# A DLRM tower with CIN layers on one core: look-ups in two passes over the tables, and part of the first copies loaded before the last features are written

## The reference

```
e = stack([tbl_f[ids[:, f]] for f in range(39)], axis=1)        # (2048, 39, 32)
conv1 = einsum('bid,bjd,ijk->bkd', e, e, W1)                    # k = 128
hidden1, final1 = conv1[:, :64], conv1[:, 64:]
conv2 = einsum('bid,bjd,ijk->bkd', e, hidden1, W2)              # k = 128
z = sum(concat([final1, conv2], 1), axis=2)                     # (2048, 192)
h = relu(concat([z, dense_ctx], 1) @ W_top1 + b_top1)           # 512
h = relu(h @ W_top2 + b_top2)                                   # 256
y = h @ W_top3                                                  # (2048, 1)
```

## Time and profile before

| | |
|---|---|
| median of 3 runs | 811.2 us (807.7 to 817.63) |
| profiled execution, its own time | 808.5 us |
| its span | 806.6 us |
| mean granted clock of TensorE | 0.966 of full |
| PE busy | 739.2 us (92%) |
| DVE busy | 697.9 us (87%) |
| ACT busy | 572.3 us (71%) |
| POOL busy | 543.3 us (67%) |
| DMA | 179.32 MB, 222 GB/s over the span |

### The profile page before, as it was taken

One profiled execution on the slowest core, in us unless ns is written; L12 is line 12 of the kernel. 1 busy time (PEld: TensorE's weight loads), 2 busy tenths in 40 slices (PEclk: granted clock), 3 DMA queues, 4 the chain that ended last, 5 costly groups with the idle time before them and its releaser, 6 DMA issues.

```text
span 806.6 us, 18279 instructions
## 1 busy us (share of the span) xinstructions
PE 739.2 (92%) x6938; PEld 431.1 (53%) x6938; DVE 697.9 (87%) x1142; ACT 572.3 (71%) x1535; POOL 543.3 (67%) x538
## 2 busy tenths in 40 slices
PE   2991787899999999999999999998999999999997
PEld 1660132375656565655556464655556565656576
DVE  6971986879999999899989898997999999999962
ACT  1330335768888888888887878786888888788883
POOL 6877777777777777777777777777777777700000
PEclk9995986899999999999999999999999999999999
DMA  6738878988898888989898889888898989888500
GB/s 194 233 66 221 241 189 235 254 244 250 253 235 248 239 257 232 262 237 247 228 255 244 243 240 242 241 235 243 232 252 237 252 234 265 248 252 249 158 2 2
DMA packets 135720, 179.32 MB, mean 222 GB/s; under 512 B 105304, under 2 KB 116518, under 8 KB 117648
## 3 DMA queue, kind: packets, MB, share of 16 engines
q1 hardware_dynamic: 111524, 166.84, 71.6%
q0 software_dynamic: 17088, 8.78, 6.6%
q10 hardware_dynamic: 7020, 2.52, 1.2%
HBM read 166.35 MB, written 16.71 MB: 227 GB/s over the span
## 4 chain that ended last, share of the span: by engine, by line
PE 29%; DVE 20%; DMA 20%; ACT 11%; SPq 8%; POOL 6%; issue 6%; ACTq 0%; DVEq 0%; POOLq 0%
DVE blocks L787 18%; DMA copies<-xt 16%; PE hidden L420 14%; SPq L350 7%; PE sums L473 6%; PE sums L447 6%; POOL emb L386 6%; ACT arena L636 5%; DMA xt<-emb 2%; DMA emb<-in_tbl,ids_tile 2%; ACT hid_high L605 2%; PE sums L478 2%; DVE turned L819 2%; ACT xdiag L624 2%; ACT hidden L613 1%
## 5 line engine op out<-in xcount | busy, mean ns | idle before, releaser
L386 POOL DMA_INDIRECT emb<-in_tbl,ids_tile x534 | 543.1, 1017 | 164.8 <-issue 112.5
L787 DVE TENSOR_TENSOR blocks<-copies 117x512 f32<-117x512 f32 x840 | 524.7, 693 | 75.5 <-DMA copies<-xt 59.7
L420 PE MATMUL hidden<-blocks,w_pairs 117*64 117x512 f32 x1792 | 434.6, 614 | 40.3 <-DVE blocks L787 38.4
L636 ACT ACTIVATE arena<-sums 64x480 f32<-64x480 f32 (+2 forms) x936 | 293.0, 313 | 138.6 <-PE sums L447 125.6
L420 PEld LDWEIGHTS hidden<-blocks,w_pairs 117*64 117x64 f32 x1792 | 152.1, 139 | 244.9 <-issue 105.5
L447 PEld LDWEIGHTS sums<-xdiag,turned 64*103 64x103 f32 x2000 | 101.5, 172 | 82.5 <-issue 46.1
L624 ACT ACTIVATE xdiag<-turned 32x468 f32<-32x468 f32 (+1 forms) x256 | 118.8, 464 | 25.7 <-DVE turned L763 22.6
L447 PE MATMUL sums<-xdiag,turned 64*103 64x78 f32 x2000 | 115.4, 262 | 3.3 <-ACT arena L636 2.2
L605 ACT ACTIVATE hid_high<-hidden 32x512 f32<-32x512 f32 x126 | 74.1, 588 | 11.6 <-PE hidden L420 9.7
L473 PE MATMUL sums<-arena,weights 128*64 128x128 f32 x1280 | 78.5, 279 | 0.0
L473 PEld LDWEIGHTS sums<-arena,weights 128*64 128x64 f32 x1280 | 71.1, 139 | 2.4
(11 more groups left out here) (50 smaller groups left out, 258.3 us busy)
## 6 DMA issues: line engine op xcount, KB each, us to landing
copies<-xt SPq DMA_DIRECT2D x448, 312.0 KB
emb<-in_tbl,ids_tile POOLq DMA_INDIRECT x534
xt<-emb SPq DMA_DIRECT2D x32, 152.0 KB
xt<-xt SPq DMA_DIRECT2D x16, 304.0 KB
xt<-emb SPq DMA_DIRECT2D x32, 104.0 KB
blocks<-hot_t SPq DMA_DIRECT2D x6, 512.0 KB, 6.1
xt<-emb SPq DMA_DIRECT2D x32, 56.0 KB
weights<-in_finals SPq DMA_DIRECT2D x1, 1728.0 KB
```

The costliest lines, as they stand in the source:

```text
L386: pool.indirect_dma_start(out=emb[u][:, f * D:(f + 1) * D], out_offset=None, in_=tables[f], in_offset=bass.IndirectOffsetOnAxis(ap=ids_til ...
L420: mm = nc.tensor.matmul(hidden[64 * c:64 * c + 64, k % 2, bank, :], w_pairs[0:ROWS, t, bank * HALF_HID:bank * HALF_HID + HID], blocks[0:RO ...
L636: op = nc.scalar.activation(out[:, :, cols].rearrange("p h (u b) -> p h u b", u=2), g[rows, i], ACT.Copy)
L787: op = nc.vector.tensor_tensor(blocks[0:ROWS, at + c, :], a[:, cols], b[:, cols], ALU.mult)
```

## The change

The 12 look-ups run in another order: j % 6 is the table and j // 6 the half, so the first six look-ups serve samples 0 to 1,023 of all six tables. They no longer skip the 128 samples of tile 0: ScalarE copies these rows into `emb[0]` (a new activation in `copy_rows`, counted in `hot_first`), and POOL's six gathers for them are gone, with the waits of the gathers on `hot_looked`. The ids are loaded in 12 pieces of 1,024 (eight places) instead of six of 2,048 (four places). All six tables are loaded at the start, each to a place of its own; five unpacked tables lie in buffers 2 and 3 of `copies`, the sixth and the raw ones in buffers 6 and 7, so the second place of the ones is buffers 4 and 5. The rows are stored to DRAM in two stores (tiles 1 to 7, tiles 8 to 15) of all six features instead of three stores of two features. On SP, the first two parts of the spill of tile 0 are issued, then, when they have landed, eight loads with those rows of copies 0, 4 and 1 that are already written (`EARLY`, 227 rows of 8 KB), then the last part of the spill, the wait for it, and the rest of the loads. In `spill` the wait for the last part's gathers moves behind the DMA L316.

```diff
-ONES_BEFORE = [2 * c for c in itertools.accumulate([0] + HOT_C)]
+ONES_BEFORE = list(itertools.accumulate([0] + HOT_C + HOT_C))
-INDICES = 4
-TABLES = 4
+INDICES = 8
+TABLES = 5
-COPIES_FREE = LOOKUPS - 8
-ONES_PLACE = [j % 3 if j < COPIES_FREE else 2 if j % 2 == 0 else 0 for j in range(LOOKUPS)]
+TURNED_FREE = LOOKUPS - 3
+ONES_PLACE = [j % 3 if j < LOOKUPS - 1 else 0 for j in range(LOOKUPS)]
+EARLY = {(0, 0): (0, 32), (0, 1): (0, 32), (0, 2): (0, 32), (4, 0): (0, 32), (4, 1): (0, 13),
+         (1, 0): (0, 30), (1, 1): (0, 30), (1, 2): (0, 26)}
...
                 for s in some:
                     part = PARTS[s]
-                    sp.wait_ge(gathered[u][s], 16 * gathers(tile, s))
+                    if s < len(PARTS) - 1:
+                        sp.wait_ge(gathered[u][s], 16 * gathers(tile, s))
                     if s == 0 and tile:
                         sp.wait_ge(hot_rows_loaded[u], 16 * hot_loads(tile))
+                    elif s == 0:
+                        sp.wait_ge(hot_first, N_HOT)
                     if s == len(PARTS) - 1:
                         sp.wait_ge(spilled_first[u], 16 * 2 * (p + 1))
                         sp.dma_start(xt[u, F:F + AGAIN, :, :].rearrange("f h n -> (f h n)").rearrange("(a b) -> a b", a=16),
                                      xt[u, 0:AGAIN, :, :].rearrange("f h n -> (f h n)").rearrange("(a b) -> a b", a=16)
                                      ).then_inc(spilled[u], 16)
+                        sp.wait_ge(gathered[u][s], 16 * gathers(tile, s))
...
-                elif chunk == 1:
-                    sp.wait_ge(hot_looked, COPIES_FREE)
-                elif v in (2, 3):
+                elif chunk == 1 or v in (2, 3):
                     sp.wait_ge(hot_looked, LOOKUPS)
                 for g, r in enumerate(ROTATION[v]):
-                    sp.dma_start(x_copy[v][k % ahead][g::THIRDS, :],
-                                 xt[u, r:r + F, k, :]).then_inc(copied[v][k % ahead], 16)
+                    skip = EARLY[v, g][1] if chunk == 0 and (v, g) in EARLY else 0
+                    sp.dma_start(x_copy[v][k % ahead][g::THIRDS, :][skip:F],
+                                 xt[u, r + skip:r + F, k, :]).then_inc(copied[v][k % ahead], 16)
+
+            def load_early():
+                sp.wait_ge(spilled_first[0], 16 * 2)
+                sp.wait_ge(spilled[0], 16 * 2)
+                sp.wait_ge(cleared, 3)
+                for (v, g), (first, last) in EARLY.items():
+                    r = ROTATION[v][g]
+                    sp.dma_start(x_copy[v][0][g::THIRDS, :][first:last],
+                                 xt[0, r + first:r + last, 0, :]).then_inc(copied[v][0], 16)
 
             def first_tile():
-                for n in range(N_HOT):
-                    index(n)
...
-                    spill(0, 0, [s for s in range(len(PARTS)) if FIRST_SPILLED[s] == n])
+                for j in range(LOOKUPS):
+                    index(j)
...
+                spill(0, 0, range(len(PARTS) - 1))
+                load_early()
+                spill(0, 0, [len(PARTS) - 1])
                 sp.wait_ge(spilled[0], 16 * SPILLS)
...
-            for f in range(F):
-                if f >= AT_ONCE:
-                    pool.wait_ge(hot_looked, (f - AT_ONCE) // A_LOOKUP + 1)
+            for f in range(N_HOT, F):
                 gather(0, f)
             pool.wait_ge(ids_loaded[1], 16)
-            for at, f in enumerate(range(N_HOT, F)):
-                pool.wait_ge(hot_looked, (F - AT_ONCE + at) // A_LOOKUP + 1)
+            for f in range(N_HOT, F):
                 gather(1, f)
...
             def look_up(j):
-                n = j // 2
+                n = j % N_HOT
...
-                        skip = P if j % 2 == 0 and bank == 0 else 0
...
             def copy_rows(j):
-                n, h = j // 2, j % 2
+                n, h = j % N_HOT, j // N_HOT
                 act.wait_ge(hot_summed, j + 1)
+                if h == 0:
+                    nc.scalar.activation(emb[0][:, n * D:(n + 1) * D], sums[:, j % 4, 0:D], ACT.Copy).then_inc(hot_first, 1)
...
-            load_table(0)
-            load_table(1)
+            for n in range(N_HOT):
+                load_table(n)
             for n in range(3):
                 unpack(n)
-                load_table(n + 2)
             act.dma_start(dense_rows[:, :, :], dense).then_inc(dense_loaded, 16)
             for j in range(LOOKUPS):
                 stage(j)
-                if j % 4 == 1 and j > 4:
-                    keep((j - 5) // 4)
+                if j == N_HOT + 1:
+                    keep(0)
                 if j:
                     copy_rows(j - 1)
-                if j % 2 == 0 and j // 2 + 3 < N_HOT:
-                    unpack(j // 2 + 3)
...
+                if j + 3 < N_HOT:
+                    unpack(j + 3)
...
             for j in range(LOOKUPS):
                 indices_to_ones(j)
-                if j % 2 and j // 2 + 2 < N_HOT:
-                    split(j // 2 + 2)
+                if j + 2 < N_HOT:
+                    split(j + 2)
...
-            dve.wait_ge(hot_looked, LOOKUPS - 1)
+            dve.wait_ge(hot_looked, TURNED_FREE)
             turn_x(0, 0)
```

More of the change, by code:

```diff
@@ L138, in build @@
         y_col = sb("y_col", [P, TILES], F32)
-        rows = sb("rows", [P, 2, TILES, 2, D], F32)
+        rows = sb("rows", [P, 2, TILES // 2, N_HOT, D], F32)
         row_number = sb("row_number", [P, 18], F32)
@@ L176, in build @@
         hot_consts_loaded = sem("hot_consts_loaded")
-        hot_raw_loaded = [sem(f"hot_raw_loaded{n}") for n in range(2)]
+        hot_raw_loaded = [sem(f"hot_raw_loaded{n}") for n in range(N_HOT)]
         hot_unpacked = sem("hot_unpacked")
@@ L185, in build @@
         hot_copied = sem("hot_copied")
+        hot_first = sem("hot_first")
         hot_kept = [sem(f"hot_kept{m}") for m in range(2)]
@@ L258, in gathers @@
             part = PARTS[s]
-            each = part.stop - max(part.start, N_HOT)
-            return each * (tile // 2 + 1) if tile % 2 else part.stop - part.start + each * (tile // 2)
+            return (part.stop - max(part.start, N_HOT)) * (tile // 2 + 1)
         def hot_loads(tile):
@@ L266, in loads_done @@
         def loads_done(u, tile, k):
-            return 16 * len(ROTATION[u]) * (tile + 1 if len(x_copy[u]) == 2 else 2 * tile + k + 1)
+            early = len([w for w, _ in EARLY if w == u]) if k == 0 or len(x_copy[u]) == 1 else 0
+            return 16 * (early + len(ROTATION[u]) * (tile + 1 if len(x_copy[u]) == 2 else 2 * tile + k + 1))
         @block.sync
@@ L278, in _, with index @@
             sp.wait_ge(hot_stored, 16)
[L280 to L283, removed]
+            def index(j):
+                if j >= INDICES:
+                    sp.wait_ge(ones_ready, ONES_BEFORE[j - INDICES + 1])
+                h = j // N_HOT
+                sp.dma_start(hot_index[j], hot_t[j % N_HOT, h * HALF_B:(h + 1) * HALF_B].partition_broadcast(P)
+                             ).then_inc(hot_index_loaded[j % INDICES], 16)
             def load_hot_rows(tile):
@@ L290, in load_hot_rows @@
                     sp.wait_ge(spilled[u], 16 * SPILLS * (tile // 2))
-                else:
-                    for m in range(2):
-                        sp.wait_ge(hot_kept[m], 16 * ((KEPT + 1 - m) // 2))
+                if tile in (1, TILES // 2):
+                    sp.wait_ge(hot_kept[tile // (TILES // 2)], 16)
                 sp.dma_start(emb[u][:, 0:N_HOT * D], hot_kept_rows[tile]).then_inc(hot_rows_loaded[u], 16)
@@ L533, in look_up @@
                     for bank in range(BANKS):
-                        skip = P if j % 2 == 0 and bank == 0 else 0
-                        mm = nc.tensor.matmul(hidden[0:3 * D, j % 2, bank, skip:512], upper[n][:, c, :],
-                                              hot_ones[j][:, c, bank * 512 + skip:(bank + 1) * 512],
+                        mm = nc.tensor.matmul(hidden[0:3 * D, j % 2, bank, :], upper[n][:, c, :],
+                                              hot_ones[j][:, c, bank * 512:(bank + 1) * 512],
                                               start=(c == 0), stop=(c == HOT_C[n] - 1))
@@ L543, in add_parts @@
                     pe.wait_ge(hot_copied, j - 3)
-                for t in range(0 if j % 2 else 1, TILES // 2):
+                for t in range(TILES // 2):
                     mm = nc.tensor.matmul(sums[:, j % 4, t * D:(t + 1) * D], staged[j % 2][:, t * P:(t + 1) * P],
@@ L690, in load_table @@
             def load_table(n):
-                if n >= 2:
-                    act.wait_ge(hot_unpacked, n - 1)
-                act.dma_start(hot_raw[n], tables[n].rearrange("(p c) d -> p c d", c=HOT_C[n])).then_inc(hot_raw_loaded[n % 2], 16)
+                act.dma_start(hot_raw[n], tables[n].rearrange("(p c) d -> p c d", c=HOT_C[n])).then_inc(hot_raw_loaded[n], 16)
             def unpack(n):
-                act.wait_ge(hot_raw_loaded[n % 2], 16 * (n // 2 + 1))
-                if n >= TABLES:
```

(7 more changed lines are left out.)

61 lines of the change are left out of this document (25 added, 36 removed).

## The result

The changed kernel takes **815.9 us** (median of 20 runs, 811.1 to 823.25), the kernel before 812.0 (20 runs, 807.7 to 818.8, run beside it). The ratio of the two is **1.0065, 95% interval 1.0043 to 1.0088**: within 2%, but slower beyond the uncertainty of the measurement, and outside the range of 797 to 813. The profiled execution took 816.95 us, with a span of 815.2. One execution of the first experiment took 1230.4 us at a granted clock of 0.56; it and one slow one of the second are left out of the ratios.

What follows compares the result with a forecast made beforehand. It took waiting for tile 0's rows, then DMA loads, then TensorE with POOL's pace leaking in, as the bounds; 2.5 us less at the start and 5 in the steady run made 811.2 into 804 us, range 797 to 813.

Steps and rivals of the forecast that it cites:

- Part 1: Look-up stage on POOL: six gathers fewer, tile 0's end at 50.8 us, POOL 7.2 us ahead to its end.
- S: Time when SP's loads of copies go on after tile 0's spill: 69 us predicted (bounds 66.5 and 73), 65.5 before.
- Part 2: Look-ups gate tile 0's spill: ones start at 15.1 us, sixth look-up's rows ready at 49.1, last rows copied at 68.5.
- Part 3: Tile 0's spill and early loads: loads go on at 69 us, chunk 1's copies land 2.5 us earlier.
- then the start gives nothing: Sign of being wrong, at the start: loads of copies going on only after 71.5 us.
- The last spill: Rival on SP's queue: the last spill part's issue blocked behind eight early loads, up to 3 us; no separate chance, within range.
- Part 4: Steady run: with POOL ahead, gather waits shrink and leak less into the copies, gaining 5 us, half of 9.7.
- the prediction's own sign of being wrong: Steady run: `turn_x` intervals staying at 43.2 us a tile without gather waits.
- the -7.5 us: Whole kernel: predicted change of the time, -2.5 us at the start and -5 in the steady run.
- the four: Rivals: full relief (799 us, 0.17), start or relief only (809 to 811, 0.25), slower (816, 0.13), last spill blocked (in range).
- Start only: Rival, start or relief only: the steady run's slow tiles are DMA's own; -2.5 us or less, 809 to 811; chance 0.25.
- The slower one: Rival in the first look-up pass: TensorE's granted clock falls during waits for ones; +4.5 us, 816; chance 0.13.

Runs made afterwards that it cites:

- the first experiment: The changed kernel with one VectorE subtraction (125x256) more behind each set of ones from the fifth on: 807.3 us, ratio 0.9952 to the kernel before.
- the second: The changed kernel with one subtraction (125x256) behind each set of ones from the fifth on, and without the eight early loads: 806.97 us, ratio 0.9949.
- the kernel with small breaks: The changed kernel, early loads kept, with a VectorE subtraction of 125x32 after every second instruction of ones from the fifth set on: 807.91 us, ratio 0.9965.
- the three kernels with small breaks: Subtractions of 125x32 after every second instruction of ones: changed kernel with early loads (0.9965), without (804.33 us, 0.9902), and the kernel before (810.35 us, 0.9998).
- the small one: A kernel of its own with only 78 POOL gathers beside VectorE's ones in runs of 16 and 48, waits ahead of every eighth: gathers held 16.32 to 17.51 us.

## Why the prediction was wrong, point by point

**Part 1 failed**: "POOL is 7.2 us ahead from there to its end". It was 7.0 behind (gathers of tile 0 end at 65.9, not 50.8; of tile 1 at 107.9, not 94; the last at 715.4). The step took the pace of a gather beside ones from before, 1.42 us, and applied it to a stage in which the ones are differently arranged: it counted 1.1 us for gathers that fall beside ones, where one of them alone was held for 17.9 us. (By its rows the pace is 1.46 us, since 39 gathers have 38 intervals, and a load is 1.45 us, not 1.46; neither changes the sum by more than 0.3 us.)

The step had named the rule that bears on this, the Trainium skill, "SBUF — State Buffer", section "SBUF: two separate sides", the "DVE blocks DMA" trap, by which VectorE in a two-port mode keeps GpSimd from writing descriptors; but it priced it as the rate of before carried on. The trace agrees with the rule, also in that DMAs of SP's queue run on (part 0 of the spill at 49.86, within the stall). That a gather is held over 45 instructions in a row the page does not say; the runs here show it. They show the hold and what ends it, not the port: that the port is the reason is the page's.

The price: the kernel with small breaks (0.9965) against the changed one (1.0065) is 1.0%, **8.1 us**, give or take 2.7 by the two intervals. In the first profile of the changed kernel S is 2.9 us later than with the breaks, and POOL's last gather 10; `turn_x` of tile 15 is 3.3 to 5.7 us later in its three profiles.

**Part 2 held.** Ones start at 15.26 (15.1), the rows of the sixth look-up are in `emb` at 49.8 (49.1), spill DMAs right behind it at 49.86; the last rows are copied at 68.9 (68.5).

**Part 3 failed by itself too**: S was given as 69, and the bound for "then the start gives nothing" was 71.5. Without the stall it is 72.6. The terms that were short: parts 0 and 1 landed 5.2 us after their issuing was done (53.4 to 58.6) instead of 3.2, and the last part 5.7 after its own instead of the 1 to 3 counted. In the prediction's own sum the early loads put S off by as much (57.5 to 66) as they spare (8.5 us). It never asked where S would be without them, and so took for a gain what its own numbers make nothing. The experiments price them at nothing (0.9952 with, 0.9949 without, where POOL is late) or at a loss of **5 us, give or take 4** (0.9965 against 0.9902, where POOL is on time). The last spill was not blocked at its issue (1.84 us against 1.27), so that rival was wrong in its place, though not in its size.

**Part 4 failed in its mechanism too**: 5 us were counted for waits for gathers that leak into the copies. In the changed kernel this could not show, since POOL was late. In the three kernels with small breaks POOL's last gather ends at 705.1, 696.7 and 704.1 us (708.4 before) and SP waits for no gather after 100 us; yet from `turn_x` of tile 2 to that of tile 15 they take 564.6, 563.1 and 564.9 us, where the kernel before takes 561.4, and VectorE waits for copies as long as before. That is the prediction's own sign of being wrong, intervals that stay at 43.2 us (here 43.3 to 43.5) without gather waits. What a POOL that is ahead seems to do is to let an earlier start stand: without early loads and with small breaks `turn_x` comes 6.1 us earlier in tile 2 and still 4.4 in tile 15, with the early loads alone 4.9 and then not at all. These are single profiles, so this is argued and not shown. What the slow tiles of the steady run come from stays open; the DMA time of the gathers is a rival that no run here excludes. SP's gather waits, 14.2 us before, were 9.1, 6.6 and 20.1 in three executions of the changed kernel: they vary too much to be read from one profile.

**The sum.** By chance the -7.5 us are what the change without its two faults gives: look-ups in two passes, breaks, no early loads, 0.9902, -8.0 us. The make-up is another: predicted were 2.5 at the start and 5 in the steady run; in the profile `turn_x` of tile 2 comes 6.1 us earlier and nothing is won behind it. With the two faults, 8.1 for the stall and 5.1 for the early loads are added (both are differences of these same ratios), +5.2 by the ratio of 1.0065.

**The rivals.** None of the four had the mechanism that made the kernel slower. "Start only" had the steady run right as far as the runs go: taking the gather waits away did not shorten it. The slower one had nearly the right time (816) and the wrong cause: TensorE's granted clock is 1.00 in the windows from 20 to 70 us, at the upper of its levels, and the look-ups end where they should. The prediction had read the Trainium skill, "TensorE: Matmul & The Clock Gate", section "HAM oscillation", as speaking for up to 16 us; the waits of TensorE in the first pass were 0.5 to 1.5 us and brought nothing. The section's example has longer waits than these, which the prediction did not weigh. The rival on the slower side should have been looked for on POOL, whose gathers the chain of waits led through.

## What to carry to other kernels

When a change rearranges work on VectorE while GpSimd issues DMAs, look at which breaks it takes away, not only at how much work it moves: ask how long the longest unbroken row of fast VectorE instructions is, and what queues on GpSimd behind it. One small instruction of another kind between them, or a wait that is long fulfilled, lets the DMAs through. And a load that is brought forward on the queue that also carries the critical transfer is worth its bytes less the delay of all that stands behind it; here that was nothing or less. Lastly, a wait that stands beside another in the profile need not cause it: make the one go away and look whether the other does.

## What the runs showed of the hardware

- A gather (`DMA_INDIRECT`) takes 0.94 us with VectorE idle, 1.28 beside ones with the next one 1.58 after it (four of the ones' 0.396), and can be held for the whole rest of an unbroken row of them: 17.9, 18.7, 19.1 us in the changed kernel, 16.3 to 17.5 in the small one.
- It doesn't seize at once: in the small kernel always one or two gathers pass before one is held, in the changed kernel two or three (counting those that begin before the row and reach into it). What decides which gather is held, the phase between the two engines or something else, stays open.
- A subtraction of 125x32 in f32 (0.18 us), one of 125x256 (0.42 us) and a fulfilled semaphore wait ahead of each instruction each let a gather in. How many waits are needed is open: one ahead of every eighth was not enough.
